# Attention in front of a mixture of experts: a tile's helper work dealt out anew over its 16 heads

## The reference

```python
def _L0_xattn_ref(q, k, v, Wc, bc):          # 16 heads of 64 in 4 groups; one key/value head per group
    scores = jnp.einsum('bghsd,bgtd->bghst', qh, kh) * scale
    probs = jax.nn.softmax(scores, axis=-1)
    out = jnp.einsum('bghst,bgtd->bghsd', probs, vh)
    return out @ Wc.T + bc
def _L0_ffn_ref(hidden_states, gate_kernel, gate_proj, up_proj, down_proj):
    routing_weights = jax.nn.softmax(x2d @ gate_kernel, axis=-1)
    routing_weights, selected_experts = jax.lax.top_k(routing_weights, 8)     # of 32 experts
    ...
x = x + _L0_xattn_ref(_layernorm(x), ctx_512, ctx_512, L0_xattn_Wc, L0_xattn_bc)
x = x + _L0_ffn_ref(_layernorm(x), ...)
```

## Time and profile before

| | |
|---|---|
| median of 3 runs | 9770.18 us (9763.78 to 9770.65) |
| profiled execution | 9766.52 us, its span 9764.4 us |
| attention stage | from about 50 to 3078 us of the span |
| busy share of the whole span | PE 94%, PEld 79%, DVE 66%, ACT 45%, POOL 54% |
| granted TensorE clock, mean | 0.975 |

### The profile page before, as it was taken

The page is one execution under the profiler, slowest core; times in us unless marked ns, Lnnn a source line. Parts: engine busy times, 40 slices in busy tenths (PEclk is TensorE's granted clock), DMA queues, the critical chain, the costliest instruction groups (busy, mean ns, idle before and its releaser), DMA issues.

```text
span 9764.4 us, 171795 instructions
## 1 busy us (share of the span) xinstructions
PE 9171.4 (94%) x44592; PEld 7700.9 (79%) x44593; DVE 6407.9 (66%) x10304; ACT 4437.6 (45%) x7458; POOL 5273.7 (54%) x5081
## 2 busy tenths in 40 slices
PE   7888888888895999999999999999999999999999
PEld 5777666667674788888888888888888888888888
DVE  6777777777775566666655666656666566656565
ACT  6666666666663333333333333333333333333333
POOL 3444444444444565666655665656665555655564
PEclk9999999999997999999999999999999999999999
DMA  2111111111112455555544555546555455555454
GB/s 88 48 50 49 53 50 48 48 50 54 47 47 63 107 112 119 126 117 113 116 106 106 129 114 111 112 107 135 113 116 110 105 110 114 132 109 112 111 124 81
DMA packets 664525, 918.17 MB, mean 94 GB/s; under 512 B 338193, under 2 KB 477457, under 8 KB 663954
## 3 DMA queue, kind: packets, MB, share of 16 engines
q0 software_dynamic: 209920, 604.72, 28.8%
q1 hardware_dynamic: 454162, 308.44, 12.1%
HBM read 1064.79 MB, written 376.45 MB: 148 GB/s over the span
## 4 chain that ended last, share of the span: by engine, by line
PE 60%; DMA 4%; issue 1%; DVE 1%; ACT 1%; SPq 1%; POOL 0%; DVEq 0%; ACTq 0%; POOLq 0%
PE bank L1520 39%; PE bank L1543 21%; DMA gu_raw<-in_L_ffn_up_proj 4%; SPq L1255 1%; ACT gu_hi L1354 1%; DVE gu_lo L1434 0%; ACT xT_hi L1347 0%; DVE h_lo L1451 0%; DVE h L1446 0%; POOL xg L1307 0%; DVE xT_lo L1428 0%; DVE h_hi L1449 0%; DVE xT L1423 0%; PE bank L1570 0%; DVEq L41 0%
## 5 line engine op out<-in xcount | busy, mean ns | idle before, releaser
L1307 POOL DMA_INDIRECT xg<-xn_rows,gather_row x2304 | 2753.5, 1195 | 2081.4 <-PE bank L1520 1452.4
L1520 PE MATMUL bank<-xT_hi,gu_hi 128*128 128x512 f32 (+2 forms) x6912 | 2553.7, 369 | 100.9 <-DVE xT_lo L1428 87.2
L1520 PE MATMUL bank<-xT_lo,gu_hi 128*128 128x512 f32 (+2 forms) x6912 | 2543.9, 368 | 0.0
L1520 PE MATMUL bank<-xT_hi,gu_lo 128*128 128x512 f32 (+2 forms) x6912 | 2543.7, 368 | 0.0
L1365 ACT ACTIVATE gated<-bank 128x512 f32<-128x512 f32 x432 | 258.4, 598 | 3042.0 <-PE bank L1520 3042.0
L1520 PEld LDWEIGHTS bank<-xT_hi,gu_hi 128*128 128x128 f32 x6912 | 1299.6, 188 | 278.0 <-issue 89.9
L1319 POOL DMA_INDIRECT out_rows<-rows_out,entry_now x576 | 1139.6, 1978 | 681.5 <-DVE rows_out L1458 322.6
L1520 PEld LDWEIGHTS bank<-xT_lo,gu_hi 128*128 128x128 f32 x6912 | 1299.8, 188 | 159.0
L1520 PEld LDWEIGHTS bank<-xT_hi,gu_lo 128*128 128x128 f32 x6912 | 1299.4, 188 | 158.6
L1446 DVE TENSOR_TENSOR h<-bank,gated 128x512 f32<-128x512 f32 x432 | 297.7, 689 | 1588.9 <-ACT gated L1365 1588.9
L1543 PE MATMUL bank<-d_hi,h_hi 128*128 128x512 f32 x3162 | 1256.0, 397 | 73.4 <-DVE h_lo L1451 73.3
(11 more groups left out here) (162 smaller groups left out, 14635.2 us busy)
## 6 DMA issues: line engine op xcount, KB each, us to landing
gu_raw<-in_L_ffn_gate_proj SPq DMA_DIRECT2D x576, 384.0 KB
gu_raw<-in_L_ffn_up_proj SPq DMA_DIRECT2D x576, 384.0 KB
d_raw<-in_L_ffn_down_proj SPq DMA_DIRECT2D x144, 1536.0 KB
xg<-xn_rows,gather_row POOLq DMA_INDIRECT x2304
x_t<-in_x SPq DMA_DIRECT2D x64, 512.0 KB, 4.8
inv_wide<-inverse_sums SPq DMA_DIRECT2D x512, 64.0 KB
out_rows<-x SPq DMA_DIRECT2D x64, 512.0 KB, 5.4
xn_rows<-xn SPq DMA_DIRECT2D x64, 512.0 KB, 6.4
```

The lines of the kernel that those rows point to most:

```text
L1307: pool.indirect_dma_start(out=xg[:, m, :], out_offset=None, in_=quarter_rows, in_offset=bass.IndirectOffsetOnAxis(ap=gather_row[:, m:m + 1 ...
L1520: last = nc.tensor.matmul(bank[:, 0:cols], w[:, c, n, j * P:(j + 1) * P], v[:, c, 0:cols], start=(c == 0 and w is gu_hi and v is xT_hi), s ...
```

## The change

The projection of tile i - 1 is spread over the heads: half n = 0 in heads 0 to 7 (its first column already at head 15 of the tile itself), half n = 1 in heads 8 to 14. The residual halves go to heads 9 and 15, the second statistics to 11 and 15. The second factors, normalisation, transposes and router go to the following tile (heads 0, 3, 4 and 5, 6), where the choice follows at 7 (copy of the logits now behind pT_lo), 11 and 13; ranks, placing, entering and the scatters go one tile further. The first normalisation is at head 6, the query split at 7, the bias addition at 8 behind `normalise_out`, the query transposes at 10 to 13. The two swapped copies of a key group go to two heads. The queries are transposed in MISC[0] alone, xn2, router and ranks use MISC[1]. A new semaphore out_read frees oT_hi by groups.

```diff
@@ -195,6 +195,7 @@
+out_read = sem("out_read")
 wo_done, x2_ready, back_chain, stats2 = sem("wo_done"), sem("x2_ready"), sem("back_chain"), sem("stats2")
@@ -218,14 +219,17 @@
-PROJECT = {1: ((0, 0, 2),), 2: ((0, 2, 4),), 3: ((0, 4, 6),), 4: ((1, 0, 2),), 5: ((1, 2, 5),),
-           6: ((0, 6, 8),), 7: ((1, 5, 8),)}
-NEXT_STATS, NEXT_NORM, NEXT_SPLIT, NEXT_QUERIES = (1, 2), 5, 6, (9, 10, 11, 12)
-RESIDUAL, STATS2, NORM2, TRANSPOSE2, ROUTER = (7, 8), (8, 9), 12, (13, 14), 15
-CHOOSE, RANKS, PLACE = (0, 1), 3, (3, 5)
-SCATTERS = {7: (0,), 8: (1,), 9: (2,), 12: (3,), 13: (4,), 14: (5,), 15: (6, 7)}
-FIRST_TILE_VALUES, FIRST_TILE_KEYS = {0: 2, 4: 3}, {2: 2, 6: 3}
-LAST_TILE_VALUES, LAST_TILE_KEYS = {8: 0, 12: 1}, {10: 0, 14: 1}
+PROJECT = {0: (1, 0, 1, 2), 1: (1, 0, 2, 3), 2: (1, 0, 3, 4), 3: (1, 0, 4, 5), 4: (1, 0, 5, 6), 7: (1, 0, 6, 8),
+           8: (1, 1, 0, 2), 9: (1, 1, 2, 3), 10: (1, 1, 3, 4), 11: (1, 1, 4, 5), 12: (1, 1, 5, 6), 13: (1, 1, 6, 7),
+           14: (1, 1, 7, 8), 15: (0, 0, 0, 1)}
+NEXT_STATS, NEXT_FACTORS, NEXT_NORM, NEXT_SPLIT, NEXT_QUERIES, NEXT_BIAS = (1, 2), 2, 6, 7, (10, 11, 12, 13), 8
+RESIDUAL, STATS2 = (9, 15), (11, 15)
+FACTORS2, NORM2, TRANSPOSE2, ROUTER, CHOOSE, MARK, TOP_EXP = 0, 3, (4, 5), 6, 7, (11, 13), 8
+RANKS, TAKE_RANKS, PLACE, ENTER = 1, 2, 3, 5
+SCATTERS = {6: 0, 7: 1, 9: 2, 10: 3, 11: 4, 12: 5, 13: 6, 14: 7}
+VALUES = {0: 2, 4: 3}, {8: 0, 12: 1}
+KEYS = {1: 2, 5: 3}, {9: 0, 13: 1}
+LAST = TILES - 1
@@ -360,11 +376,15 @@
-    def queries_lo(i, s):
+    def queries_lo(i):
...
                            xq[:, :, 0, :].bitcast(F32), ALU.subtract).then_inc(xq_ready, 1)
+    def add_bias(i, s):
+        hold(xn_ready, i + 1)
         pool.tensor_tensor(x_t[s][:, :], x_t[s][:, :], bias_row[:, :], ALU.add).then_inc(xbias_ready, 1)
@@ -393,26 +413,32 @@
         for h in range(H):
+            if h in SCATTERS and t.back3:
+                hold(pthi_copied, H * t.i + h + 1)
+                scatter(t.i - 3, (SCATTERS[h],))
             if h in OUT_SUM and (t.back1 or not OUT_SUM[h][0]):
                 normalise_out(t.i - OUT_SUM[h][0], OUT_SUM[h][1])
-            if h == 2 and t.next:
+            if h == FACTORS2 and t.back2:
+                factors2(t.i - 2)
+            if h == NEXT_FACTORS and t.next:
                 factors1(t.i + 1)
-            if h == 6 and t.next:
-                queries_lo(t.i + 1, t.next_s)
-            if h in SCATTERS and t.back2:
-                hold(pthi_copied, H * t.i + h + 1)
-                scatter(t.i - 2, SCATTERS[h])
-            if h == 10 and t.back1:
-                factors2(t.i - 1)
+            if h == NEXT_SPLIT and t.next:
+                queries_lo(t.i + 1)
+            if h == NEXT_BIAS and t.next:
+                add_bias(t.i + 1, t.next_s)
...
     factors1(0)
-    queries_lo(0, 0)
+    queries_lo(0)
+    add_bias(0, 0)
     all_tiles(pool, tile)
     for g in (G - 2, G - 1):
-        normalise_out(TILES - 1, g)
-    scatter(TILES - 2, range(TOP_K))
-    factors2(TILES - 1)
-    scatter(TILES - 1, range(TOP_K))
+        normalise_out(LAST, g)
+    factors2(LAST - 1)
+    scatter(LAST - 2, (0, 1, 2))
+    factors2(LAST)
+    scatter(LAST - 2, range(3, TOP_K))
+    scatter(LAST - 1, range(TOP_K))
+    scatter(LAST, range(TOP_K))
     pool.wait_ge(table_written, 16 * TOP_K * TILES)
@@ -470,7 +496,9 @@
         act.wait_ge(onorm_ready, G * i + g + 1)
-        if g == 0:
+        if g < G - 1:
+            wait(act, out_read, (G - 1) * (i - 1) + g + 1)
+        else:
             wait(act, wo_done, NH * i)
@@ -506,23 +534,22 @@
                 split_out_hi(i - OUT_SPLIT[h][0], OUT_SPLIT[h][1])
-            for b, g, is_values in values_and_keys_at(t, h):
-                if is_values:
-                    values_hi(b, g)
-                else:
-                    copy_keys(b, g)
-            if h == CHOOSE[0] and t.back2:
-                top_exponent(i - 2)
+            for b, g in groups_at(t, h, VALUES):
+                values_hi(b, g)
+            for b, g in groups_at(t, h - 1, KEYS):
+                copy_keys(b, g)
+            if h == NORM2 and t.back2:
+                normalise2(i - 2)
+            if h in TRANSPOSE2 and t.back2:
+                copy_xn2(i - 2, TRANSPOSE2.index(h))
             if h == NEXT_NORM and t.next:
...
                 queries_hi(i + 1)
+            if h == TOP_EXP and t.back2:
+                top_exponent(i - 2)
             if h in NEXT_QUERIES and t.next:
                 copy_queries(i + 1, t.next_s, NEXT_QUERIES.index(h))
-            if h == NORM2 and t.back1:
-                normalise2(i - 1)
-            if h in TRANSPOSE2 and t.back1:
-                copy_xn2(i - 1, TRANSPOSE2.index(h))
@@ -566,11 +594,11 @@
-    def copy_keys_swapped(b, g):
+    def copy_keys_swapped(b, g, half):
         dve.wait_ge(kt_copied, G * b + g + 1)
-        for to, at in ((0, HEAD_DIM), (HEAD_DIM, 0)):
-            dve.tensor_copy(kT_swapped[to:to + HEAD_DIM, g, :], O_BANK[g % 2][at:at + HEAD_DIM, :]
-                            ).then_inc(kts_copied, 1)
+        to, at = ((0, HEAD_DIM), (HEAD_DIM, 0))[half]
+        dve.tensor_copy(kT_swapped[to:to + HEAD_DIM, g, :], O_BANK[g % 2][at:at + HEAD_DIM, :]
+                        ).then_inc(kts_copied, 1)
@@ -641,24 +669,32 @@
                                      iota_e[:, :].unsqueeze(1).to_broadcast([P, TOP_K, E]), ALU.is_equal))
+        assert chain.n == 1
+    def choice(j):
         with nc.allow_low_precision(reason="a sum of one 1 at most"):
...
                               ).then_inc(chosen_ready, 1)
-        assert chain.n == 1
-    def place(j):
+    def take_ranks(j):
...
         dve.wait_ge(rank_done, j + 1)
-        chain.then(dve.tensor_tensor(pos[:, :], MISC[1][:, 0:E], slot_base[:, :], ALU.add))
-        chain.then(dve.tensor_tensor(slot_base[:, :], MISC[1][:, E:2 * E], slot_base[:, :], ALU.add))
+        chain.then(dve.tensor_tensor(pos[:, :], turned(j, 0)[:, 0:E], slot_base[:, :], ALU.add))
+        chain.then(dve.tensor_tensor(slot_base[:, :], turned(j, 0)[:, E:2 * E], slot_base[:, :], ALU.add))
         dve.sem_inc(rank_copied, 1)
+        assert chain.n == 2
+    def place(j):
+        chain = Chain(dve, back_chain, BACK_STEPS * j + 6)
         chain.then(dve.tensor_tensor(hot_pos[:, :, :], hot[:, :, :],
...
             chain.then(dve.tensor_reduce(slot_i[:, :], hot_pos[:, :, :], AX.X, ALU.add))
-        assert chain.n == 4
+        assert chain.n == 2
@@ -674,36 +710,40 @@
         for h in range(H):
-            if h == CHOOSE[0] and t.back2:
-                copy_logits(i - 2)
             if h + AHEAD < H:
...
                 maximum(i + 1, h + AHEAD - H)
+            for b, g in groups_at(t, h - 2, KEYS):
+                copy_keys_swapped(b, g, 1)
             if h in INVERT:
                 invert(i, INVERT[h])
-            if t.back2:
-                if h == CHOOSE[0]:
-                    choose(i - 2)
-                if h == CHOOSE[1]:
-                    mark(i - 2)
             copy_probs_lo(i, h)
...
                 split_out_lo(i - OUT_SPLIT[h][0], OUT_SPLIT[h][1])
-            for b, g, is_values in values_and_keys_at(t, h):
-                if is_values:
-                    values_lo(b, g)
-                else:
-                    copy_keys_swapped(b, g)
-            if t.back2:
-                if h == PLACE[0]:
-                    place(i - 2)
-                if h == PLACE[1]:
-                    enter(i - 2)
+            for b, g in groups_at(t, h, VALUES):
+                values_lo(b, g)
+            for b, g in groups_at(t, h - 1, KEYS):
+                copy_keys_swapped(b, g, 0)
+            if t.back3:
+                if h == TAKE_RANKS:
+                    take_ranks(i - 3)
+                if h == PLACE:
+                    place(i - 3)
+                if h == ENTER:
+                    enter(i - 3)
             if h in NEXT_STATS and t.next:
                 statistics1(i + 1, t.next_s, NEXT_STATS.index(h))
+            if t.back2:
+                if h == CHOOSE:
+                    copy_logits(i - 2)
+                    choose(i - 2)
+                if h == MARK[0]:
+                    mark(i - 2)
+                if h == MARK[1]:
+                    choice(i - 2)
             if t.back1 and h in RESIDUAL:
@@ -738,14 +780,14 @@
-        if n >= 2:
-            pe.wait_ge(qt_copied, 4 * i + n - 1)
+        if n >= 1:
+            pe.wait_ge(qt_copied, 4 * i + n)
         elif isinstance(i, int) and i == 1:
-            pe.wait_ge(qt_copied, n + 3)
+            pe.wait_ge(qt_copied, 4)
         else:
-            wait(pe, x2_ready, 2 * (i - 2) + n + 1)
+            wait(pe, x2_ready, 2 * (i - 2) + 1)
         for k in range(4):
-            last = nc.tensor.transpose(MISC[n % 2][:, k * P:(k + 1) * P].bitcast(F32R),
+            last = nc.tensor.transpose(MISC[0][:, k * P:(k + 1) * P].bitcast(F32R),
```

(54 more changed lines are left out.)

83 lines of the change are left out of this document (49 added, 34 removed).

## The result

The changed kernel takes 9939.61 us (median of 4 runs, 9936.25 to 9942.34); beside it the kernel before took 9769.0. The ratio is 1.0178, 95% interval 1.0165 to 1.0191: **slower by 1.8%**, 170 us, where the prediction said 9728 and at most 9830. Lines shift: neg_max L577 is now L605, pT_lo L591 is L619, oT_lo L605 is L633, the cast of the choice L636 is L664, the residual L616 is L644, the query split L366 is L382, the bias addition L368 is L388, o_norm L381 is L401, scatter L389 is L409, scores L771 and L772 are L813 and L814, the query transposes L748 are L790.

The account below looks back on a forecast made before the run. VectorE's in-order chain across engines was taken as the bound. Tiles -46 us (batch 183.9 against 187.0), start -4 and tail +8 sum to -42: 9728 us against the median, range 9630 to 9830.

Parts of the forecast that it names:

- the walk over its steps: VectorE, inner tile: base steps 32.2 us and helpers 9.2 make 41.4; with waits and the bias lock, 44.2 us.
- the bias lock: Head 9: oT_lo (L605) waits until GpSimd's bias addition ends, on a shared SBUF port pair; +1.6 us per tile.
- The wait behind the first normalisation: Head 6: VectorE waits for ScalarE's pT_hi copy behind the normalisation, with enter no longer filling the time; +0.9 us.
- mark is free of it: Mark moves to head 11, where GpSimd only scatters, so the lock gives back 0.4 us, already in its 0.46 price.
- the router's wait at head 15: VectorE's wait for the router at the tile's boundary goes, as the router moves to head 6; saves 1.9 us.
- the argument that the cast has one input: Head 7: given, with no row showing such an overlap, against the cast being held by GpSimd's query split.
- the price of a last and a first tile: Inner tile plus key and value group costs: last tile 47.9 us (was 50.0), first 47.6 (was 47.8).
- rival (c): Head 7: the cast takes the shared port and waits for the query split; 2.2 us per tile, 9858 us; 12%.
- rival (b): TensorE's in-order queue waits at heads 4, 5, 6 and 10; 0.7 us per tile for VectorE gives 9770; 17%.
- The tail: Last pT_lo to the schedule: scatters of three tiles instead of two, 57.0 to 65 us, +8 (bounds +4 and +15).
- The start: Third tile leaves out ranks, place and enter, 2.7 us, the second also choose and mark; -4 us in all.
- The lost cover: Heads 0 and 1: choose and mark no longer run while ScalarE makes the exponent and o_low; 1.5 us, counted in 41.4.

Follow-up runs that it names:

- e3: Changed kernel with the bias addition moved to head 14 and the cast to head 11, directly ahead of its reader: 9754.16 us, ratio 0.9987.
- e9: e1 with the cast still at head 7, but written as a reduction over a dimension of length 1 instead of a copy: 9739.08 us, ratio 0.9966.
- e2: Changed kernel with only the cast moved, from head 7 to head 11: 9843.24 us, ratio 1.0076.
- e1: Changed kernel with only the bias addition moved, from head 8 to head 14: 9818.27 us, ratio 1.0052.
- e6: Kernel before the change with its loop over batches written out: 9701.92 us, ratio 0.9932.
- e5: e3 with its loop over batches written out: 9665.37 us, ratio 0.9892.
- e12: e8 with the loop over batches written out and enter moved to head 6 ahead of pT_lo: 9588.47 us, ratio 0.9819.
- e8: e3 with four VectorE helpers (first statistics half, enter, choose, choice) moved ahead of the sums of heads 0, 4, 8, 12: 9706.13 us, ratio 0.994.
- e7: Kernel before the change with only the bias addition moved, to behind normalise_out of head 8: 9786.37 us, ratio 1.0021.
- e10: e7 with the second residual moved from head 8 to 9 and second statistics from 8 and 9 to 9 and 10: 9926.92 us, ratio 1.0169.
- e4: Changed kernel with its loop over batches written out: 9795.43 us, ratio 1.0028.

## Why the prediction was wrong

**What held.** The chain on VectorE bounds the stage, and the walk over its steps was right to about 1 us: without the bias lock it gave 42.6 us for an inner tile, e3 has 43.5. The wait behind the first normalisation, put down as +0.9 at head 6, is 0.8 us in step 7: right in size, one head later, since pT_hi of head 6 is copied ahead of the normalisation. The lock of the bias addition on oT_lo of head 9 came as put down, +1.6 us per tile predicted, 1.5 measured (step 9), and mark is free of it at head 11 (hot now 0.42 us). In the inner tiles the router's wait at head 15 is gone: that step is 2.88 us with residual and statistics in it.

**What failed.** The prediction has 183.9 us for a batch; the changed kernel takes 52.8 + 45.4 + 48.9 + 51.8 = 198.9. Over 59 tiles, 14.75 batches, the 15.0 us are 221, and with the ends (below) 224; the miss is 212 us by the medians and 218 by the profiled executions. Two steps failed: the argument that the cast has one input and so is not held (6.6 of the 15.0 us), and the price of a last and a first tile, built without the branch back (6.5).

- **The rival (c) came true, and the forecast had it at 12%.** In s = 2 and s = 0 the cast is held by the query split, 2.8 and 2.1 us, not at all in s = 1 and 3. The step that failed is "Against: it has one input". e9 shows what decides: not the number of inputs but that it is a copy. The forecast's own look at the times had found the two operations 0.2 us apart, and in first tiles in the wrong order; so close a race should have had far more than 12%. Rival (c)'s price, 2.2 us in each tile and 130 in all, was too high, since 29 of the 64 casts are held: the cast's place is worth 96 us beside the other lock (e2) and 64 without it (e1 to e3). Of the 15.0 us per batch 6.6 are this: e3, without both locks, takes 12.6 less per batch than the changed kernel, of which 6.05 (three times 1.6, and 1.25 in the last tile) had been predicted for the other lock.
- **The late residual.** Part of these 6.6 us is what the locks do to TensorE: rival (b) named the query transposes at head 10 waiting for the residual of head 9. They did wait, 3.54 us in s = 2 and s = 0 and 1.84 in s = 1, and after the long stop the clock was low: step 11 in s = 2 and s = 0 is 1 us longer than in s = 1. e1 brings the stop to 2.08 us and takes the cost away in s = 2 (3.64 to 2.57), not in s = 0 (3.59 to 3.37), where e2 does (2.86); why the two kinds differ is open. It is a bill for VectorE's stop paid by another engine two heads later, and the sum had no term for it.
- **The last and first tiles were built up from the inner tile**, so they left out what sits in them alone: the gap of the branch back, 3 us in the last tile. It was in the measured 50.0 us of the earlier trace rows and the prediction, at 47.9, took it away without an edit that removes it. Nor was the 1.9 us of the router's wait to be had there: in e6, without the branch, step 15 of s = 3 is 1.62 us and holds no wait for the router. e3 has 51.1 and 48.1 where the prediction without the lock gives 46.7 and 46.0: 4.4 and 2.1 of the 15.0 us; with the loop written out (e5) the two tiles are 3.8 and 1.7 us shorter, an inner tile 0.7.
- **The remaining 1.8 us per batch** are 0.9 in each inner tile (43.5 against 42.6), in small waits of steps 5, 7, 11 and 15.
- **The ends.** The tail was put at +8 and is +1.2: the scatters of three tiles do lie there, but the router and the choice of the tile before the last run beside them. The start was put at -4 and the first four tiles are 6.0 us later, in e3 only 1.0: the locks again.

The lost cover (1.5 us per tile) was right in kind: e12 with helpers ahead of the sums is 77 us below e5. But e8, with 48 us, shows that it can't be had in full by itself.

So where did the expected gain go? The new order without the two locks does shorten the inner tile, by 1.0 us (e3); no run separates the projection's part in it from the router's. The change brought two of VectorE's operations beside GpSimd's 2.4 us operations, and these cost three times that, 3.15 us per tile (12.6 per batch).

## What to carry to other kernels

When helper work is dealt out anew, write down for each long GpSimd operation which VectorE operations can start while it runs, and count copies and casts from SBUF to SBUF among the exposed ones, however small, as well as operations with two SBUF inputs; move one of the two, or give the small one another form. A lock costs only what VectorE is too early by, so the same pair can cost 0.3 us a tile in one order (e7) and 1.5 in another (e10). A tile of special kind is priced from its own measured length, with what the change takes out of it, not from the plain tile with additions.

## What the runs showed that was not expected

- A cast of 128x8 elements took up to 2.87 us. An operation with one input in SBUF and one in a bank was free beside the same split: in the kernel before the residual ran inside it in 62 tiles and took 0.68 us each time. The cast was held even where its record starts 0.39 us ahead of the query split's (1150.36 and 1150.75), while a scatter was still running on GpSimd; in s = 3 a cast that starts 0.33 us ahead took 0.29 us, and in s = 1, 0.12 us ahead, 0.17. A record's start does not say who got the port; what does is not settled here.
- The branch back of a loop whose body is four tiles costs VectorE a gap of 3.1 us and ScalarE one of 2.4. The Trainium skill, "Runtime: NRT & Kernel Launch", section "Instruction fetch mechanics", says that a taken branch to a target outside the instructions at hand waits for them to be fetched; the gap, gone in e4, agrees, but no run here shows the fetch itself. The loop written out gave 66 us to the kernel before and 89 to e3.
- After a stop of 3.5 us TensorE ran at 1.2 GHz for some 4 us, and a lock between VectorE and GpSimd was thus paid a second time.
